# Projecting q, k and v of a tile in one stage, with 64-row remainders in pairs, in a vision-transformer block on one Trainium2 core

## The chip, the core and the metric

The kernel runs on one core of one Trainium2 chip. The metric is the time of one launch on the device in microseconds (us). The kernel before took 1381.76 us, the median of three runs (1381.58 to 1386.32). A core has five engines with a queue each: TensorE (PE, with its weight loads shown as PEld), VectorE (DVE), ScalarE (ACT), GpSimd (POOL) and SyncE (SP), which issues most transfers. Each engine works its own instructions off in the written order and waits on semaphores that others raise.

## The reference

64 images of 3x224x224 become 14x14 patches of 768 values. One transformer block follows, 12 heads of 16 channels, with layer norms; its feed-forward part rounds activations and weights to small integers.

```python
hidden = einsum('npd,hd->nph', patches, W_lin) + b_lin     # 768 -> 192
h = concat([cls_tok, cls_token, hidden])                   # 198 tokens an image
q, k, v = split(layernorm(h) @ w_qkv.T, 3)                 # 192 -> 576
q, k = rope(q * scale), rope(k)
out = softmax(q @ k.T) @ v                                 # 12 heads of 16
h = h + out @ w_proj.T + b_proj
up, gate = split(bitlinear(layernorm(h), w_in, g_in), 2)   # 192 -> 2 * 512
h = h + bitlinear(silu(gate) * up, w_out, g_out)           # 512 -> 192
```

## The kernel before

The 64 x 198 tokens are one row of 12672, cut into 99 tiles of 128 tokens. Attention works by image: 3 groups of 4 heads each, 192 groups in all. A loop over steps `s` (119 of them) stands in the program of each engine; a step embeds tile `s` (on PE `embed`, L427: 6 chunks of 128 rows by 192 columns) and works on earlier tiles and images at the same time. `half_steps` gives the half step at which each group's scores are maximised (`MAX_AT`), exponentiated and weighed (`EXP_AT`) and at which an image is normalised (`OUT_AT`); `projection_steps` gives the step of the feed-forward part of a tile (`PROJ_AT`). The order of the stages within a step is written out by hand at the end of each engine's program.

The way of a tile: PE embeds it, DVE adds the bias (L841) and takes the statistics (L845, L847), POOL normalises (`norm_x`, L984 to L991), PE transposes it (L437) as two blocks of 96 channels, ACT copies them to `xT` (L643), a ring of five images. `project_qk` (L446) makes q and k: two products over 96 rows each, 384 columns wide. `project_v` (L501) makes v by image: four products of 192 columns for the two halves of 99 tokens, since `weigh_values` (L513) needs the values of an image with its tokens on partitions 0 to 98. POOL turns q and k (`rotate`, L1003 to L1010), PE transposes them (L456), ACT copies (L661), POOL rounds a copy (L1019). PE multiplies scores for the row maximum (`max_scores`, L469) and again for the exponential (`exp_scores`, L490), for four heads at once, each on 32 of the 128 rows of the array; `weigh_values` puts four heads on 32 columns each. The negated maximum goes through a transposition (L478), a copy (L668) and a transfer of SP (`place_max`, L342) into `qkT`. After that come L522 (transposed output), L862 and L866 (normalised), L532, `project_out` (L539, L540), the residual (L872), the quantisation, `transpose_xr` (L547), `ffn_in` (L558: two products over 96 rows for each of two halves of 512 columns, bf16), `tanh_gate` (L716), `gated` (L903, L909), `transpose_yr` (L566) and `ffn_out` (L576).

Both kinds of scores use one set of four accumulator banks in turn: `take_score` makes PE wait until DVE (L854) or ACT (L675) has read what was there. All other outputs go to four banks `turn`, given out by `take` in the order of the program: the bank that was used longest ago, after a wait for its last reader. Products in 4-byte floats are two MATMUL instructions each in the trace, products in bf16 and transpositions one.

After the last tile is embedded (step 98), `keep_busy` (L414) adds four idle products a step.

Of the kernel before, what the change touches and what calls it, by code (L numbers as in the profile page):

```python
# [14 lines left out]
IMGS = 64  # L15
# [9 lines left out]
DC = D // 2  # L25
HEADS = 12
# [20 lines left out]
XRING = 5 * TOKENS  # L47
# [30 lines left out]
VALUE_AT = [EXP_AT[GROUPS * b] - 2 for b in range(IMGS)]  # L78


def projection_steps():
    steps = []
    for i in range(TILES):
        steps.append(max(steps[-1] + 1 if steps else 0, (OUT_AT[final_image(i)] + 3) // 2))
    return steps
# [3 lines left out]
STEPS = PROJ_AT[-1] + 8  # L89
# [38 lines left out]
X_COPIES = copies(TILES, TILE, XRING)  # L128
# [10 lines left out]
def build(nc, ins, out):  # L139
# [3 lines left out]
    with ExitStack() as ctx:  # L143
# [10 lines left out]
        wqkv = sb("wqkv", [DC, 2, 3 * D])  # L154
        wproj = sb("wproj", [DC + 1, 2, D])
        win = sb("win", [DC, 2, 2 * FF])
        wout = sb("wout", [128, FC, D])
        winq = sb("winq", [DC, 2, 2 * FF], BF16)
# [6 lines left out]
        wabs = sb("wabs", [128, 2])  # L165
# [9 lines left out]
        xT = sb("xT", [DC, 2, XRING + TILE])  # L175
# [8 lines left out]
        vaug = sb("vaug", [TT, 2, 2, HEADS, 32])  # L184
# [22 lines left out]
        xiT = sb("xiT", [DC, TBUF, 2, TILE], BF16)  # L207
# [30 lines left out]
        margin_loaded = sem("margin_loaded")  # L238
        bias_loaded = [sem(f"bias_loaded{p}") for p in range(BBUF)]
# [10 lines left out]
        qk_ready = sem("qk_ready")  # L250
# [13 lines left out]
        v_ready = sem("v_ready")  # L264
        v_copied = sem("v_copied")
        pv_ready = sem("pv_ready")
# [32 lines left out]
        ATTN_LOADS = 16 * 4  # L299
        FFN_LOADS = 16 * 6  # L300
        SUM_STEP = 5
# [6 lines left out]
        def _(sp):  # L308
# [20 lines left out]

            def load_rope(i):  # L330
# [6 lines left out]

            def place_max(b):
# [5 lines left out]

            def store(i):
# [5 lines left out]
            load(0)  # L351
            load_bias(0)
            load(1)
            for i in range(1, BBUF):
                load_bias(i)
            for i in range(TBUF):
                load_rope(i)
            load(2)
            for s in range(STEPS):
                for i in tile_at(s + 1):  # L360
                    if beyond(i) > TOKENS - PATCHES:
                        load_margin(i)
                    if i >= BBUF:
                        load_bias(i)
                for b in range(IMGS - XSLOT):
                    if final_tile(b) == s - 1:
                        load(b + XSLOT)
                for i in tile_at(s - 2):
                    if i >= TBUF:
                        load_rope(i)  # L370
                for i in at(PROJ_AT, s - 7):
# [3 lines left out]
                for b in at(NMAX_AT, 2 * s + 1):  # L375
                    place_max(b)
            for p in range(TBUF):
# [3 lines left out]
        def _(pe):  # L381
# [3 lines left out]
            def take(use, size, freed, count):  # L385
# [7 lines left out]
                bank_of[use] = k  # L393
                return k

            def take_score(freed, count):
                if score_freed[0] is not None:
                    pe.wait_ge(*score_freed[0])
                score_freed[0] = (freed, count)

            score_freed = [None]

            def weight_sums():
                pe.wait_ge(setup_dve, 3)
                k = take("win", 1, weights_ready, 1)
                pe.matmul(turn[:, k, 0:1], ones[0:DC, :], wabs[0:DC, 0:1], start=True, stop=True).then_inc(wsum_ready, 1)
# [9 lines left out]
            def embed(i):  # L416
                if i == 0:
                    pe.wait_ge(loaded_embed, 16)
                    pe.wait_ge(x_zeroed, XSLOT + 1)
                for b in range(first_image(i), final_image(i) + 1):  # L420
                    pe.wait_ge(x_loaded[b % XSLOT], 16 * (b // XSLOT + 1))
# [704 lines left out]
```

## Time and profile before

| | us |
|---|---|
| median of 3 runs | 1381.76 |
| the profiled execution | 1382.6 |
| its span, first to last instruction | 1380.8 |
| PE busy | 1327.5 (96%) |
| POOL busy | 1012.3 (73%) |
| DVE busy | 975.0 (71%) |
| ACT busy | 904.8 (66%) |
| first embedding of the last tile to the end | 161 |

The mean granted clock of TensorE was 0.986 of full speed. Engines overlap, so the busy times don't add up to the span. A busy PE isn't PE at its peak: the time of a stage is best read as the distance from its first instruction to the first of the next stage.

### The profile page before, as it was taken

How to read it: one execution, taken by the hardware profiler on the slowest of the kernel's cores; microseconds unless marked ns; L12 is line 12 of the kernel's file. 1: busy time of each engine (PE TensorE's matmuls, PEld its weight loads, DVE VectorE, ACT ScalarE, POOL GpSimd, SP SyncE). 2: the span in 40 equal slices, each digit the busy share in tenths (PEclk: the TensorE clock that was granted, in tenths of full speed). 3: DMA queues.
4: the chain of work that ended last, by engine and by line, in shares of the span. 5: the costliest groups of instructions: out<-in, count | busy, mean ns of one | idle time of the engine just before them, and what ended most of it. 6: DMA issues, size and time to landing. Idle time of an engine off the chain costs nothing.

```text
span 1380.8 us, 37853 instructions
## 1 busy us (share of the span) xinstructions
PE 1327.5 (96%) x13274; PEld 980.4 (71%) x13274; DVE 975.0 (71%) x2318; ACT 904.8 (66%) x1606; POOL 1012.3 (73%) x1610
## 2 busy tenths in 40 slices
PE   3899999999999999999999999999999999999997
PEld 2666777777777777777777777777777777767666
DVE  0644777777777777777787777777777777777765
ACT  0145667676777776767767767767767776767664
POOL 2655777887777787877878877778778778877544
PEclk8899999999999999999999999999999999999999
DMA  5421112221121221222122111211111221100000
GB/s 156 109 51 47 34 50 59 58 55 37 53 62 36 58 53 43 54 67 55 39 60 56 53 41 49 64 53 39 52 49 46 65 58 32 44 12 11 11 15 22
DMA packets 127119, 69.28 MB, mean 50 GB/s; under 512 B 50741, under 2 KB 126358, under 8 KB 126838
## 3 DMA queue, kind: packets, MB, share of 16 engines
q1 hardware_dynamic: 125884, 64.08, 17.7%
q10 hardware_dynamic: 1050, 2.79, 0.7%
q8 instruction: 110, 1.80, 0.6%
q14 instruction: 75, 0.61, 0.2%
HBM read 56.48 MB, written 9.73 MB: 48 GB/s over the span
## 4 chain that ended last, share of the span: by engine, by line
PE 89%; DVE 3%; SPq 2%; DMA 2%; ACT 2%; issue 2%; POOL 1%; DVEq 0%; POOLq 0%; ACTq 0%
PE turn L427 14%; PE score L490 12%; PE turn L513 11%; PE turn L446 10%; PE turn L558 6%; PE turn L501 6%; PE score L469 5%; PE turn L456 4%; PE turn L566 4%; PE turn L539 3%; PE turn L522 3%; PE turn L437 2%; PE turn L540 2%; PE turn L576 2%; PE turn L547 2%
## 5 line engine op out<-in xcount | busy, mean ns | idle before, releaser
L854 DVE TENSOR_REDUCE nmax<-score 99x8 f32<-99x1584 f32 x192 | 346.9, 1807 | 77.4 <-PE score L469 77.3
L675 ACT ACTIVATE prob<-score 99x1584 f32<-99x1584 f32 x192 | 286.6, 1493 | 95.9 <-PE score L490 95.9
L1019 POOL CAST qkTr<-qkT 128x768 fp32r<-128x768 f32 (+15 forms) x114 | 110.2, 973 | 198.5 <-ACT qkT L661 198.5
L427 PE MATMUL turn<-wlin,xp 128*128 128x192 f32 x1188 | 220.1, 337 | 24.9 <-DMA xp<-in_x 17.5
L427 PEld LDWEIGHTS turn<-wlin,xp 128*128 128x128 f32 x1188 | 199.6, 197 | 30.7 <-issue 30.7
L490 PE MATMUL score<-qkT 17*99 17x198 f32 x3072 | 179.2, 347 | 4.6 <-DVE nmax L854 4.5
L513 PE MATMUL turn<-prob,vaug 99*32 99x198 f32 x3072 | 167.4, 337 | 0.0
L446 PE MATMUL turn<-wqkv,xT 96*128 96x384 f32 x396 | 156.5, 519 | 0.0
L490 PEld LDWEIGHTS score<-qkT 17*99 17x99 f32 x3072 | 115.8, 160 | 51.3 <-issue 50.3
L1024 POOL TENSOR_SCALAR ve<-mv 128x1 f32<-128x1 f32 x99 | 123.1, 1243 | 32.8 <-DVE mv L847 24.9
L1033 POOL TENSOR_TENSOR yg<-y,gout 128x512 f32<-128x512 f32 x99 | 125.8, 1271 | 9.7 <-ACT yr L737 8.2
L692 ACT ACTIVATE osb<-turn 128x198 f32<-128x198 f32 x192 | 64.7, 337 | 81.2 <-PE turn L513 79.3
L513 PEld LDWEIGHTS turn<-prob,vaug 99*32 99x32 f32 x3072 | 80.6, 109 | 41.3 <-issue 15.9
L903 DVE SCALAR_TENSOR_TENSOR ag<-th,turn 128x512 f32<-128x512 f32 x99 | 68.1, 688 | 58.2 <-ACT th L716 58.2
L1003 POOL TENSOR_TENSOR ropec<-qk,rope 128x384 f32<-128x384 f32 x99 | 99.3, 1003 | 10.7 <-ACT qk L651 10.5
L1010 POOL TENSOR_TENSOR qkp<-ropec,ropes 128x384 f32<-128x384 f32 x99 | 99.2, 1002 | 7.8
L446 PEld LDWEIGHTS turn<-wqkv,xT 96*128 96x128 f32 x396 | 69.1, 193 | 50.4 <-issue 24.8
L558 PE MATMUL turn<-winq,xiT 96*128 96x512 bf16 x396 | 101.6, 378 | 0.0
L1005 POOL TENSOR_TENSOR ropes<-qk,rope 128x384 f32<-128x384 f32 x99 | 100.4, 1014 | 0.0
L708 ACT ACTIVATE xiT<-turn 96x256 bf16<-96x256 f32 x99 | 37.6, 380 | 89.6 <-PE turn L547 89.6
L841 DVE TENSOR_TENSOR h<-turn,bias 128x192 f32<-128x192 f32 x99 | 35.4, 357 | 83.5 <-PE turn L427 64.0
L501 PE MATMUL turn<-wqkv,xT 96*99 96x192 f32 x512 | 93.9, 326 | 0.0
(98 smaller groups left out, 2694.2 us busy)
## 6 DMA issues: line engine op xcount, KB each, us to landing
xp<-in_x SPq DMA_DIRECT2D x64, 588.0 KB, 4.7
out<-h SPq DMA_DIRECT2D x99, 96.0 KB, 2.0
qkT<-nmaxT SPq DMA_DIRECT2D x192, 3.1 KB
bias<-in_added SPq DMA_DIRECT2D x30, 74.2 KB
win<-in_win ACTq DMA_DIRECT2D x1, 768.0 KB
wlin<-in_wlin ACTq DMA_DIRECT2D x1, 576.0 KB, 3.8
rope<-in_cos SPq DMA_DIRECT2D x30, 6.2 KB
rope<-in_sin SPq DMA_DIRECT2D x30, 6.2 KB
```

The lines of the kernel that those rows point to most:

```text
L427: last = pe.matmul(turn[:, k, 0:D], xp[:, c, place:place + TILE], wlin[:, c, :], start=(c == 0), stop=(c == KC - 1))
L446: last = pe.matmul(turn[:, k, 0:QK], xT[:, c, place:place + TILE], wqkv[:, c, 0:QK], start=(c == 0), stop=(c == 1))
L490: last = pe.matmul(score[0:TT, r, t * TOKENS:(t + 1) * TOKENS], qkT[rows, GROUPS + g, place + t * TT:place + (t + 1) * TT], qkT[rows, g, p ...
L501: last = pe.matmul(turn[0:TT, k, t * D:(t + 1) * D], xT[:, c, place + t * TT:place + (t + 1) * TT], wqkv[:, c, QK:3 * D], start=(c == 0), ...
L513: last = pe.matmul(turn[32 * r:32 * r + 32, k, 0:TOKENS], vaug[:, b % 2, t, hd, :], prob[:, t, hd, :], start=(t == 0), stop=(t == 1), skip ...
L558: last = pe.matmul(turn[:, k + half, :], xiT[:, i % TBUF, c, :], winq[:, c, half * FF:(half + 1) * FF], start=(c == 0), stop=(c == 1))
L675: act.activation(prob[:, :, 4 * g:4 * g + 4, :].rearrange("p t r n -> p r t n"), score[0:TT, :, 0:2 * TOKENS].rearrange("p r (t n) -> p r ...
L854: dve.tensor_reduce(nmax[:, b % 2, :, 4 * g:4 * g + 4].rearrange("p t r -> p r t"), score[0:TT, :, 0:2 * TOKENS].rearrange("p r (t n) -> p ...
L1005: pool.tensor_tensor(ropes[:, :].rearrange("p (h e f) -> p h e f", e=DH // 2, f=2), src[:, :, :, ::-1], sin, ALU.mult).then_inc(rope_parts, 1)
L1019: pool.tensor_copy(qkTr[:, :, place:place + n], qkT[:, :, place:place + n]).then_inc(qkT_rounded, 1)
L1024: pool.tensor_scalar(ve2[:, c], mv2[:, i % TBUF, 1:2], 1.0 + NORM_EPS, LN_EPS * NORM_EPS, ALU.mult, ALU.add).then_inc(norm2, 1)
L1033: pool.tensor_tensor(yg[:, i % 2, :], y[:, i % 2, :], gout[:, :], ALU.mult).then_inc(yg_ready, 1)
```

## The change

- `project` replaces `project_qk` and `project_v`. For each tile it makes two outputs in two banks, 288 columns each: q with the first half of v, k with the second half of v. The 192 channels are taken as 128 rows and 64 rows. `xT` and the weights now hold channels 0 to 127 in chunk 0 and channels 64 to 191 in chunk 1. Side 0 takes its 128 rows from chunk 1 and its remaining 64 from rows 0 to 63 of chunk 0; side 1 takes chunk 0 and rows 64 to 127 of chunk 1. So the two remainders lie on different halves of the array's rows.
- `ffn_in` is cut the same way: `whole` (two products over 128 rows, 512 columns) and `rest` (two over 64 rows).
- `rest_first` puts the remainders first if the stage just before ended with remainders; otherwise they come last.
- v is copied by tile (`copy_v`, with a 1 behind the 16 channels of each head) and moved by SP (`place_v`, 2 or 3 transfers a tile) to `vaug`, a ring of six images, with a head every 17 columns; `weigh_values` reads 32 columns from there.
- The transposed tile is used one step after its embedding, not three; scores start two steps earlier. `exps` runs a half step later after the maximum, `transpose_max` in the same half step as the last maximum.
- The order within a step is remade on every engine. On PE both `weigh_values` stand together, `transpose_yr` comes five steps after `project_out` (four before) and `ffn_out` seven (four before), `project` is near the end of the step.
- At the start the image and weights of the embedding are loaded in halves, SP loads images ahead of most biases, the attention's weights come in 19 loads instead of 4, and the loads of the feed-forward weights are issued in step 4 by ACT instead of at the start.

```diff
-            top.append(max(top[-1] + 1 if top else 0, 2 * (final_tile(b) + 5) + 2))
-        turn.append(top[-1] + 1)
+            top.append(max(top[-1] + 1 if top else 0, 2 * (final_tile(b) + 3) + 2))
+        turn.append(top[-1])
         for g in range(GROUPS):
-            soft.append(max(soft[-1] + 1 if soft else 0, turn[-1] + 1))
-        out.append(soft[-1] + 2)
+            soft.append(max(soft[-1] + 1 if soft else 0, turn[-1] + 2))
+        out.append(soft[-1] + 3)
...
+            def project(i):
+                pe.wait_ge(xT_copied, i + 1)
+                k = take(("qkv", i), 2, v_copied, i + 1)
+
+                def whole(start, stop):
+                    for side in range(2):
+                        last = pe.matmul(turn[:, k + side, 0:SIDE], xT[:, i % 2, 1 - side, :], wqkv[:, 1 - side, side, :],
+                                         start=start, stop=stop)
+                    return last
+
+                def rest(start, stop):
+                    for side in range(2):
+                        rows = slice(side * REST, (side + 1) * REST)
+                        last = pe.matmul(turn[:, k + side, 0:SIDE], xT[rows, i % 2, side, :], wqkv[rows, side, side, :],
+                                         start=start, stop=stop)
+                    return last
+
+                if rest_first():
+                    rest(True, False)
+                    whole(False, True).then_inc(qkv_ready, 1)
+                else:
+                    whole(True, False)
+                    rest(False, True).then_inc(qkv_ready, 1)
...
+            def place_v(i):
+                sp.wait_ge(v_copied, i + 1)
+                over = (TILE * (i + 1) - 1) // TOKENS - VRING
+                if over >= 0:
+                    sp.wait_ge(pv_ready, GROUPS * (over + 1))
+                for p, half, at, n in token_runs(i):
+                    b = (TILE * i + p) // TOKENS
+                    sp.dma_start(vaug[at:at + n, b % VRING, half, 0:VROW], vt[p:p + n, i % VSLOT, :])\
+                        .then_inc(v_placed[i % VSLOT], 16)
...
-            for s in range(STEPS):
+            for s in range(-2, STEPS):
                 if s == SUM_STEP + 1:
                     weight_sums()
-                for b in at(OUT_AT, 2 * s - 2):
-                    transpose_on(b)
                 for n in at(MAX_AT, 2 * s):
                     max_scores(n)
-                for i in tile_at(s - 3):
-                    transpose_xn(i)
+                for b in at(OUT_AT, 2 * s - 1):
+                    transpose_on(b)
                 for i in tile_at(s):
                     embed(i)
-                if s >= TILES + LATE:
-                    keep_busy(s)
-                for i in at(PROJ_AT, s - 1):
-                    transpose_xr(i)
+                for i in tile_at(s - 1):
+                    transpose_xn(i)
                 for b in at(OUT_AT, 2 * s):
                     transpose_o(b)
+                for i in at(PROJ_AT, s - 7):
+                    ffn_out(i)
                 for b in at(NMAX_AT, 2 * s):
-                    transpose_max(b)
-                for b in at(NMAX_AT, 2 * s + 1):
                     transpose_max(b)
                 for n in at(EXP_AT, 2 * s):
                     exp_scores(n)
                 for i in at(PROJ_AT, s):
                     project_out(i)
-                for i in tile_at(s - 5):
+                for i in tile_at(s - 3):
                     transpose_qk(i)
+                if s >= TILES + LATE:
+                    keep_busy(s)
+                for i in at(PROJ_AT, s - 2):
+                    transpose_xr(i)
+                for n in at(MAX_AT, 2 * s + 1):
+                    max_scores(n)
+                for n in at(EXP_AT, 2 * s - 2):
+                    weigh_values(n)
                 for n in at(EXP_AT, 2 * s - 1):
                     weigh_values(n)
-                for n in at(MAX_AT, 2 * s + 1):
-                    max_scores(n)
-                for n in at(EXP_AT, 2 * s):
-                    weigh_values(n)
-                for i in at(PROJ_AT, s - 4):
+                for i in at(PROJ_AT, s - 5):
                     transpose_yr(i)
-                for i in at(PROJ_AT, s - 1):
+                for b in at(OUT_AT, 2 * s + 1):
+                    transpose_o(b)
+                for i in at(PROJ_AT, s - 2):
                     ffn_in(i)
-                for b in at(VALUE_AT, 2 * s):
-                    project_v(b)
-                for b in at(VALUE_AT, 2 * s + 1):
-                    project_v(b)
                 for n in at(EXP_AT, 2 * s + 1):
                     exp_scores(n)
-                for i in tile_at(s - 3):
-                    project_qk(i)
-                for b in at(OUT_AT, 2 * s - 1):
+                for i in tile_at(s - 1):
+                    project(i)
+                for b in at(OUT_AT, 2 * s):
                     transpose_on(b)
-                for b in at(OUT_AT, 2 * s + 1):
-                    transpose_o(b)
-                for i in at(PROJ_AT, s - 4):
-                    ffn_out(i)
+                for b in at(NMAX_AT, 2 * s + 1):
+                    transpose_max(b)
```

## Rows read from the trace of the kernel before

**Rows 1.** Windows: stretch, length, PE PEld DVE ACT POOL busy, clock, DMA share, GB/s.
```profile
0.00:20.00 20.00, 3.61 (x12) 3.35 (x12) 1.21 (x8) 0.00 (x0) 5.12 (x15) 0.90 0.77 209
20.00:40.00 20.00, 12.47 (x42) 11.50 (x43) 2.70 (x9) 1.66 (x2) 3.08 (x8) 0.68 0.36 90
40.00:60.00 20.00, 16.03 (x89) 13.10 (x88) 12.35 (x20) 4.89 (x10) 16.23 (x20) 0.92 0.46 126
...
200.00:1190.00 990.00, 987.10 (x10105) 725.92 (x10105) 741.07 (x1773) 694.99 (x1239) 777.74 (x1231) 1.00 0.20 52
...
1340.00:1381.00 41.00, 30.96 (x194) 25.49 (x192) 25.33 (x85) 19.48 (x40) 19.25 (x43) 0.96 0.06 20
```
**Rows 2.** The longest of PE's waits from 200 to 1190 us: total, times, longest.
```profile
PE turn L478 <- DVE h L841: 1.1, 3, 0.4
```
**Rows 3.** Timeline of PE: embeddings of tiles 3, 20 and 96.
```profile
34.34 1.94 PE L427 MATMUL turn<-wlin,xp 128*128 128x192 f32 x5 [6.47 <-issue]
...
208.52 2.12 PE L427 MATMUL turn<-wlin,xp 128*128 128x192 f32 x12
...
1194.46 2.12 PE L427 MATMUL turn<-wlin,xp 128*128 128x192 f32 x12
```
**Rows 4.** Timeline of PE, one steady step: start, length, line, operands.
```profile
703.67 0.38 PE L547 MATMUL turn<-ident,xr 128*96 128x128 f32 x2
703.89 0.34 PE L478 MATMUL turn<-ident,nmax 99*12 99x99 f32 x2
704.15 0.93 PE L490 MATMUL score<-qkT 17*99 17x198 f32 x16
705.01 0.59 PE L539 MATMUL turn<-wproj,onT 96*128 96x192 f32 x2
705.44 0.49 PE L540 MATMUL turn<-wproj,onT 97*128 97x192 f32 x2
705.77 0.82 PE L456 MATMUL turn<-ident,qkp 128*128 128x128 f32 x6
706.52 0.88 PE L513 MATMUL turn<-prob,vaug 99*32 99x198 f32 x16
...
708.99 1.03 PE L558 MATMUL turn<-winq,xiT 96*128 96x512 bf16 x4
709.85 1.46 PE L501 MATMUL turn<-wqkv,xT 96*99 96x192 f32 x8
711.15 1.45 PE L446 MATMUL turn<-wqkv,xT 96*128 96x384 f32 x4
712.44 0.51 PE L532 MATMUL turn<-ident,on 99*96 99x99 f32 x4
```
**Rows 5.** Timeline of PE: a `project_qk` that follows scores.
```profile
686.45 1.56 PE L446 MATMUL turn<-wqkv,xT 96*128 96x384 f32 x4
687.85 0.49 PE L576 MATMUL turn<-woutq,yiT 128*128 128x192 bf16 x4
```
**Rows 6.** Windows of the scores at 704.15 alone: PE busy (instructions that touch it).
```profile
704.14:704.20 0.06, 0.05 (x4) 1.00 0.00 0
...
704.38:704.44 0.06, 0.06 (x8) 1.00 0.00 0
```
**Rows 7.** Timeline of PE near the end: scores, then the next use of their banks.
```profile
1303.99 0.93 PE L490 MATMUL score<-qkT 17*99 17x198 f32 x16
...
1306.62 0.43 PE L469 MATMUL score<-qkTr 16*99 16x198 f32 x8 [0.93 <-ACT prob L675]
```
**Rows 8.** Line of the copy of v: busy us, mean ns, idle before, releaser.
```profile
L683 ACT ACTIVATE vaug<-turn 99x384 f32<-99x384 f32 x64 | 31.4, 491 | 40.5 <-PE turn L501 40.5
```
**Rows 9.** Waits of SP's queue: total us, times, longest.
```profile
SPq L342 <- ACT nmaxT L668: 581.2, 64, 22.3
```
**Rows 10.** Timeline of SP at the start: transfers that it issues.
```profile
3.04 17.64 SPq L327 DMA_DIRECT2D bias<-in_added  x7
...
29.64 1.24 SPq L313 DMA_DIRECT2D xp<-in_x  x2
```

More of the change, by code:

```diff
@@ L263, in build @@
         exp_done = sem("exp_done")
-        v_ready = sem("v_ready")
         v_copied = sem("v_copied")
+        v_placed = [sem(f"v_placed{p}") for p in range(VSLOT)]
         pv_ready = sem("pv_ready")
@@ L328, in load_bias, with prepare @@
                         .then_inc(bias_loaded[i % BBUF], 16)
+            def prepare(i):
+                if beyond(i) > TOKENS - PATCHES:
+                    load_margin(i)
+                if i >= BBUF:
+                    load_bias(i)
+                for b in range(1, IMGS - XSLOT):
+                    if final_tile(b) == i - 2:
+                        load(b + XSLOT)
             def load_rope(i):
@@ L393, in take @@
                 bank_of[use] = k
+                before[0], latest[0] = latest[0], use
                 return k
@@ L493, in exp_scores @@
                 last.then_inc(st_ready, 1)
-            def project_v(b):
-                pe.wait_ge(xT_copied, X_COPIES[final_tile(b)])
-                k = take(("v", b), 1, v_copied, b + 1)
-                place = TOKENS * b % XRING
-                for t in range(2):
-                    for c in range(2):
-                        last = pe.matmul(turn[0:TT, k, t * D:(t + 1) * D], xT[:, c, place + t * TT:place + (t + 1) * TT],
-                                         wqkv[:, c, QK:3 * D], start=(c == 0), stop=(c == 1))
-                last.then_inc(v_ready, 1)
             def weigh_values(n):
@@ L507, in weigh_values @@
                 pe.wait_ge(exp_done, n + 1)
[L508 removed]
+                for i in range(TOKENS * b // TILE, final_tile(b) + 1):
+                    pe.wait_ge(v_placed[i % VSLOT], 16 * runs_loaded(i, VSLOT))
                 k = take(("pv", n), 1, o_copied, n + 1)
@@ new lines, in _ @@
+            act.wait_ge(setup_pool, SETUP_POOL)
+            for s in range(-2, STEPS):
+                if s == SUM_STEP - 3:
+                    load_ffn()
+                for i in tile_at(s - 2):
+                    copy_v(i)
+                for b in at(OUT_AT, 2 * s - 1):
+                    copy_onT(b)
+                for b in at(NMAX_AT, 2 * s - 1):
+                    copy_maxT(b)
+                for i in at(PROJ_AT, s - 5):
+                    round_y(i)
+                for i in at(PROJ_AT, s - 3):
+                    sum_squares(i)
+                for i in tile_at(s - 1):
+                    copy_xT(i)
@@ L930, in _ @@
             dve.memset(ones[:, :], 1.0).then_inc(setup_dve, 1)
-            for s in range(STEPS):
+            for s in range(-2, STEPS):
                 if s == SUM_STEP:
```

302 lines of the change are left out of this document (160 added, 142 removed).

## The prediction

> **What bounds the kernel now.** I read the windows first. From 200 to 1190 us PE is busy for 987.1 of 990 us at the full clock of 2.4 GHz, while POOL, the next, has 777.7 us [rows 1]. Then the waits: in that stretch the longest of PE's waits on another engine comes to 1.1 us in total [rows 2]. So three quarters of the span are PE's own work, and a microsecond taken from it there is one gained, until another engine's chain is late. The start differs: from 0 to 60 us PE is idle for 16.4, 7.5 and 4.0 us, 27.9 in all, and the clock is low in part [rows 1]. The last 41 us have 10.0 us idle. A steady step takes (1194.46 - 208.52) / 76 = 12.97 us on average, from the embedding of tile 20 to that of tile 96 [rows 3].
>
> **PE's columns.** The timeline gives the price of a stage as the distance to the next one [rows 4]. L446 holds four instructions of 384 columns and takes 712.44 - 711.15 = 1.29 us, so 0.84 ns a column and instruction (a product in 4-byte floats is two of them). L501, eight of 192 columns, takes 711.15 - 709.85 = 1.30 us. L558, four of 512 in bf16, takes 0.86 us, 0.215 each.
>
> Before, q, k and v cost a tile 1.29 + 64/99 x 1.30 = 2.13 us. After, the 128-row products are four instructions of 288 columns, 4 x 0.242 = 0.97 us. The remainders are four more, two sides at a time if row halves run side by side: 2 x 0.242 = 0.48 us. Sum 1.45, so 0.68 us less a tile, 67 us for 99. `ffn_in` goes from four instructions to two and a pair, three times 0.215: 0.215 less, 21 us.
>
> Do 64-row halves run side by side? No row shows one. The nearest is L490, four 32-row heads at once: 16 instructions of 198 columns would take 16 x 0.166 = 2.66 us in a row and take 0.86 [rows 4]. Within it four start at once (4 in the first 0.06 us) and the next four about 0.24 us on (8 touch the stretch from 704.38) [rows 6]: waves of four, in which the second pass of a head doesn't hold up the first pass of the next. Two row halves are the same with two members, and each side has its own bank. I take full overlap. The other end is none: 2 x 0.242 + 0.215 = 0.70 us a tile lost, 69 us.
>
> The Trainium skill ("TensorE: Matmul & The Clock Gate", Part 3) says that matmuls start and end strictly in program order. If the two passes of a side stand next to each other in the program, that makes three rounds of the pair instead of two in `project`, 0.24 us a tile. By it the sum would be 24 us higher. The waves of the scores speak against it.
>
> **Changes of array mode.** A stage of part-array products costs more than its columns. L490's four waves are 0.665 us and it takes 0.86, 0.19 more; L446 takes 1.40 us behind scores [rows 5] against 1.29 behind a full-array stage, 0.11 more; and 0.09 more stands ahead of scores (L456 takes 0.75 us for six products [rows 4], and at the price of L547, 0.22 for two, it would be 0.66). In and out together are 0.39 us, 0.195 a change. "TensorEngine Tiling (Array Packing)" of the Trainium skill, Key Properties, says that a change of mode drains the engine; it gives no time, and it is the rule that speaks against this change. What the price is here, the rows say.
>
> So I count changes in both orders of PE. Before, a steady step has in order 32-row, full, 32-row (exp), full, columns, 32-row, columns, full, 32-row (exp), full: 10 changes. After: 32-row, full, exp, full, 32-row, columns (both `weigh_values` together), full, 64-row, exp, full, 64-row, and then 32-row at once in one step of three, or by a full-array transposition first in two of three: 11 or 12. `rest_first` is nearly never true, since scores stand between the two stages with remainders. Over all steps, with the half steps that slip, the lists give 959 changes before and 1124 after. 165 x 0.195 = +32 us. A change from 64 to 32 rows isn't in the trace. At nothing, the 131 of these would take 26 us off; I take the full price, since columns to rows and back also costs (two `weigh_values` with scores between them).
>
> The full-array transpositions (L437, L547) now write 128 rows rather than 96 with the same columns: 0.
>
> **New waits in the steady part.** The pipeline is shortened and PE runs faster, so I laid out one step with the durations of the rows.
> - Score banks. After `exp_scores` starts, ACT starts 1.0 us later and takes 1.49; the next use of the banks came 1306.62 - 1303.99 = 2.63 us after, when it did wait [rows 7]. The new order puts 0.86 + 0.43 + 0.33 + 0.75 + 0.22 = 2.59 us between (L490, L539, L540, L456, L547) [rows 4]. A wait of 0.04.
> - `ffn_in` takes a bank that `copy_yiT` frees. In one step of three a transposition of the output lies between it and `transpose_yr`, and there the pair needs that bank some 0.4 us too early: 0.13 a step.
> - Transposed tile one step after embedding rather than three. DVE's and POOL's parts (L841 to L847, then `norm_factor` and L984 to L991 behind `round_qkT`) end about 0.5 us into the next step by this layout; PE asks for them at 2.3 to 2.9. Hidden, with about 2 us of slack. POOL's work is 777.7 / 990 of a step of 12.97, 10.2 us of the new 12.6, and it must still wait for the copy of `qkT` in the middle.
> - v by SP. ACT copies 192 columns a tile, where L683 copied 384 an image in 491 ns [rows 8]. Even at 491 that is 49 us for 31, 0.2 a step on an engine with 695 of 990 us busy; I take nothing. SP's queue waits 581 us for `nmaxT` [rows 9], so two or three more issues a step hide, also for the stores and image loads queued with them. The values are wanted four steps after they are copied; DMA share is 0.20. Without that cover each late transfer would stand ahead of `weigh_values`.
> In sum about 0.17 us a step, 76 + some 15 steps: +15 us. From below the waits can't be less than 0; from above I take 0.6 a step, 55 us, the point at which the slack of each chain is gone.
>
> **Start and end.** At the start SP hung 17.6 us in the issues of seven biases, and the third image was issued at 29.64 [rows 10]. After, the images stand ahead and 1.5 MB of feed-forward weights are out of the way, so tiles 1 to 3 can be embedded some 10 us earlier; but the attention's weights, 19 issues, are now needed at step 1 rather than 3. After that each tile hangs on POOL (rotation, rounding, norm), so PE idles there as before. Of the 27.9 us idle I take 12 back (bounds 0 and 22). The tail has the same number of steps; two more of them are light feed-forward steps that hang on a chain through all engines: +2 (bounds -3 and 8).
>
> **Sum.** -67 - 21 + 32 + 15 - 12 + 2 = -51. The profiled execution took 1382.6 us, its span 1380.8; the median is 1381.8. From the median: 1331 us.
>
> **Rivals.**
> 1. The pairs don't overlap at all. Speaks for it: no row has 64-row products. Against: the waves. Then -67 - 21 + 69 = -19, with 32 for the changes, 15 for waits and -10 at the ends: +18, 1400 us, slower. It decides where less than a quarter of the 0.70 us is hidden.
> 2. Program order binds within the fp32 pair: three rounds, +24 us, 1355. For: the two passes of a side use the same rows. Against: the waves.
> 3. The shortened chain (embedding, statistics, `norm_x` at the end of POOL's step, transposition in the next, `project`, `rotate`) is late in each step, or DVE behind `gated` frees `ffin`'s banks late. For: POOL has 10.2 us of work in 12.6. Against: 2 us of slack. At 0.6 us a step instead of 0.17: 1331 + 39 = 1370. If the chain sets the step at 12.97 us, it is about 1371 too, since only start and end gain.
> 4. The change from 64 to 32 rows is free, or the start gives 22: 1331 - 26 = 1305.
> 5. Beyond the layout: with a step of 13.3 us on waits of the remade order, 1400.
>
> **How the numbers follow.** Forecast as told (1315 to 1350): 0.56. Rival 4: 0.12. Rival 2: 0.07. Rival 3: 0.14. Rival 1: 0.06. Rival 5: 0.05. The range goes from rival 4 less the better start (1305 - 8 = 1297) to rival 3 (1372) and leaves out 0.14. A measurement of this kernel tells 0.5% (7 us) from no change. Faster by more: all of 4, 2 and the forecast, and most of 3 (0.10): 0.85. Within it: 0.04. Slower: 0.11.
>
> **What would show it.** In the profile after: `project`'s stage at about 1.45 us of columns plus about 0.3 for changes, and its four remainder instructions in two waves; `ffn_in` at 0.65 plus 0.2. Steady steps of 12.6 us on average. PE still above 97% busy from 200 us on, with waits for the exponential and for `copy_yiT` of about 15 us in all. Embedding of tile 3 at 24 us or earlier rather than 34.34 [rows 3]. It would be wrong if the remainders come one after the other, if PE waits for `xn` or for banks in every step, or if POOL's busy share goes to 90% and more while PE's falls.

## The result, and the profile after

The changed kernel takes 1357.6 us (median of 4, 1357.0 to 1358.4) against 1381.7 us beside it: a ratio of 0.982, interval 0.980 to 0.984. It is faster, by 24 us where 51 were forecast. Medians here and below are of fast runs: one execution with both halves on the same rows and one with twice the filler took over 1.5% more than the fastest of their kernels and are left out. The span of the profiled execution is 1356.2 us, the mean granted clock 0.974 (0.986 before).

The windows of the changed kernel (stretch, length, then busy us and instructions of PE, PEld, DVE, ACT and POOL, granted clock, DMA share, GB/s):

```profile
0.00:20.00 20.00, 8.05 (x29) 6.53 (x30) 2.10 (x11) 1.67 (x2) 6.67 (x19) 0.88 0.65 181
20.00:40.00 20.00, 17.55 (x99) 12.67 (x99) 3.71 (x10) 5.41 (x12) 14.67 (x23) 0.95 0.62 165
40.00:60.00 20.00, 12.94 (x67) 9.48 (x67) 7.94 (x11) 3.64 (x8) 8.73 (x13) 0.74 0.24 64
...
200.00:1190.00 990.00, 977.09 (x10295) 707.57 (x10293) 782.47 (x1825) 712.28 (x1295) 703.55 (x1273) 1.00 0.24 61
1190.00:1250.00 60.00, 55.47 (x581) 39.60 (x578) 42.47 (x99) 38.91 (x68) 37.94 (x61) 0.91 0.05 16
1250.00:1300.00 50.00, 42.85 (x433) 31.29 (x436) 29.39 (x79) 29.59 (x51) 15.23 (x32) 0.83 0.04 12
1300.00:1340.00 40.00, 30.33 (x203) 22.71 (x200) 29.11 (x93) 21.73 (x46) 18.95 (x41) 0.87 0.04 13
1340.00:1357.00 17.00, 14.30 (x98) 12.41 (x95) 5.72 (x17) 6.12 (x11) 4.64 (x12) 1.00 0.12 36
```

They answer to [rows 1]. The middle is as it was forecast to be: PE busy for 98.7%, at the full clock but for the ten us from 475 us on (granted 0.66). What is new is the end. Before, the stretches at the same times ran at the full clock:

```profile
1190.00:1250.00 60.00, 58.56 (x603) 42.32 (x601) 43.50 (x100) 42.36 (x77) 48.29 (x79) 1.00 0.05 13
1250.00:1300.00 50.00, 48.19 (x533) 34.49 (x530) 37.19 (x87) 36.44 (x60) 31.98 (x46) 1.00 0.03 10
```

The first question is where the stages stand. Timeline of PE in the changed kernel, part of a steady step (start, length, line, operands), which answers to [rows 4]:

```profile
705.97 0.59 PE L611 MATMUL turn<-winq,xiT 128*128 128x512 bf16 x2
706.50 0.39 PE L618 MATMUL turn<-winq,xiT 64*128 64x512 bf16 x2
706.81 0.93 PE L552 MATMUL score<-qkT 17*99 17x198 f32 x16
707.67 1.24 PE L494 MATMUL turn<-wqkv,xT 128*128 128x288 f32 x4
708.84 0.76 PE L501 MATMUL turn<-wqkv,xT 64*128 64x288 f32 x4
709.53 0.43 PE L531 MATMUL score<-qkTr 16*99 16x198 f32 x8
```

`project` is L494 and L501, 709.53 - 707.67 = 1.86 us from start to start. Of this 1.45 are columns, as forecast, and 0.41 belong to its changes of array mode (0.3 was expected there). `ffn_in` is L611 and L618, 706.81 - 705.97 = 0.84 us (forecast 0.65 + 0.2). The embedding of tile 20 starts at 216.9 us and that of tile 96 at 1174.4: a step of 957.5 / 76 = 12.60 us, the forecast's 12.6.

Do the two halves run at once? L501 holds the four remainder instructions of that stage. Its windows (stretch, length, PE and PEld busy with the number of instructions that touch it, clock, DMA share, GB/s):

```profile
708.90:708.96 0.06, 0.06 (x2) 0.06 (x4) 1.00 0.09 9
...
709.10:709.16 0.06, 0.06 (x2) 0.04 (x2) 1.00 0.10 10
709.20:709.26 0.06, 0.06 (x4) 0.00 (x0) 1.00 0.07 7
...
709.40:709.46 0.06, 0.06 (x2) 0.00 (x0) 1.00 0.10 10
```

Two instructions are under way from the first tenth of a microsecond on, four where one wave ends and the next begins, then two again: two waves of two.

**Where the 51 us went.** PE's idle time was 53.3 us and is 66.8. From 0 to 200 us it fell by 4.1 (34.7 to 30.6), from 200 to 1190 us it rose by 10.0 (2.9 to 12.9), behind 1190 us by 7.6 (15.7 to 23.3). PE's busy time fell by 38.1 us. The clock explains why not by more. Take for each window its length times what is missing of the full clock: behind 1190 us that was 1.6 us before and is 60 x 0.09 + 50 x 0.17 + 40 x 0.13 = 19.1 now, in the middle nothing and now 10 x 0.34 = 3.4, from 0 to 160 us 16.8 and now 13.8. So the work of PE fell by about 38.1 + 17.5 + 3.4 - 3.0 = 56 us (an estimate, since some of the low clock falls on idle time), where the sum had -67 - 21 + 32 = -56. In one line: work -56, middle +10 idle and +3 clock, start -4 idle and -3 clock, end +8 idle and +17.5 clock, together -24. The end costs 25 us where +2 were forecast.

The times of single tiles can't be compared in this way. Tile 20 is embedded at 216.9 us and was at 208.5, although steps are shorter, since the shortened pipeline has PE do more of the work (12 us by its busy time) ahead of that point; that work is then missing behind the last tile.

Timeline of PE in the changed kernel near the end (in brackets the idle time before, and who ended it):

```profile
1224.51 0.50 PE L643 MATMUL turn<-woutq,yiT 128*128 128x192 bf16 x4
1226.21 1.11 PE L552 MATMUL score<-qkT 17*99 17x198 f32 x16 [1.20 <-DVE nmax L929]
1227.24 1.01 PE L592 MATMUL turn<-wproj,onT 96*128 96x192 f32 x2
...
1237.53 0.43 PE L531 MATMUL score<-qkTr 16*99 16x198 f32 x8 [1.44 <-ACT prob L735]
```

The last tile has been embedded and projected by then. Between `max_scores` (L531) and the `exp_scores` (L552) whose banks DVE's row maximum frees, only L585 and L643 stand; PE waits 1.20 us. Behind the wait the clock is at the lower of its two levels, 1.2 GHz (0.84 is granted from 1220 to 1245 us): L592 takes 1227.24 to 1228.05, 0.81 us, where it took 0.43 in the steady step of before [rows 4]. `keep_busy` (L457), the filler, stands behind `transpose_qk` in the new order, past the scores. That gave the theory for the first experiment.

### The profile page after: what moved, and what is told of

It is laid out like the page before. It is cut to its first block, busy times and chain, and to the rows that moved or that the text cites. A ratio compares the mean times of both kernels' runs of the same rounds, so it can differ in the third digit from the quotient of the medians.

```text
span 1356.2 us, 38149 instructions
## 1 busy us (share of the span) xinstructions
PE 1289.4 (95%) x13160; PEld 937.5 (69%) x13160; DVE 998.7 (74%) x2319; ACT 899.5 (66%) x1629; POOL 898.8 (66%) x1610
## 4 chain that ended last, share of the span: by engine, by line
PE 85%; DVE 4%; SPq 3%; DMA 3%; ACT 2%; issue 2%; POOL 1%; ACTq 1%; DVEq 0%; POOLq 0%
PE turn L475 14%; PE score L552 11%; PE turn L566 10%; PE turn L494 8%; PE score L531 5%; PE turn L501 4%; PE turn L518 4%; PE turn L633 4%; PE turn L611 4%; PE turn L592 3%; PE turn L575 3%; PE turn L618 2%; PE turn L593 2%; PE turn L457 2%; PE turn L643 2%; PE turn L585 2%
## 5 line engine op out<-in xcount | busy, mean ns | idle before, releaser
L1094 POOL CAST qkTr<-qkT 128x768 fp32r<-128x768 f32 (+15 forms) x114 | 86.4, 764 | 206.6 <-ACT qkT L721 206.6
L552 PE MATMUL score<-qkT 17*99 17x198 f32 x3072 | 180.5, 349 | 6.5 <-DVE nmax L929 5.6
L1108 POOL TENSOR_TENSOR yg<-y,gout 128x512 f32<-128x512 f32 x99 | 137.2, 1386 | 34.3 <-ACT yr L797 20.6
L566 PE MATMUL turn<-prob,vaug 99*32 99x198 f32 x3072 | 151.0, 336 | 0.0
L552 PEld LDWEIGHTS score<-qkT 17*99 17x99 f32 x3072 | 116.6, 162 | 44.6 <-issue 44.0
L494 PE MATMUL turn<-wqkv,xT 128*128 128x288 f32 x396 | 125.1, 440 | 2.5 <-ACT xT L703 2.3
L566 PEld LDWEIGHTS turn<-prob,vaug 99*32 99x32 f32 x3072 | 90.9, 110 | 33.3 <-issue 2.4
L776 ACT ACTIVATE th<-turn,fxh 128x512 f32<-128x512 f32 x99 | 68.1, 687 | 54.3 <-PE turn L618 54.3
L518 PE MATMUL turn<-ident,qkp 128*128 128x128 f32 x594 | 83.5, 277 | 14.1 <-ACT vt L744 8.5
L494 PEld LDWEIGHTS turn<-wqkv,xT 128*128 128x128 f32 x396 | 68.4, 192 | 39.1 <-issue 25.2
L703 ACT ACTIVATE xT<-turn 128x256 f32<-128x256 f32 x99 | 38.0, 384 | 82.9 <-PE turn L485 82.9
L531 PE MATMUL score<-qkTr 16*99 16x198 f32 x1536 | 84.5, 293 | 8.6 <-ACT prob L735 8.4
```

Source lines behind the costliest of these rows:

```text
L494: last = pe.matmul(turn[:, k + side, 0:SIDE], xT[:, i % 2, 1 - side, :], wqkv[:, 1 - side, side, :], start=start, stop=stop)
L518: last = pe.transpose(turn[:, k + side, g * TILE:(g + 1) * TILE], qkp[:, i % 2, head:head + 4, :].rearrange("p h d -> p (h d)"), ident[:, :])
L531: last = pe.matmul(score[0:TT, r, t * TOKENS:(t + 1) * TOKENS], qkTr[rows, g, place + t * TT:place + (t + 1) * TT], qkTr[rows, GROUPS + g, ...
L552: last = pe.matmul(score[0:TT, r, t * TOKENS:(t + 1) * TOKENS], qkT[rows, GROUPS + g, place + t * TT:place + (t + 1) * TT], qkT[rows, g, p ...
L566: last = pe.matmul(turn[32 * r:32 * r + 32, k, 0:TOKENS], vaug[:, b % VRING, t, VHEAD * hd:VHEAD * hd + 32], prob[:, t, hd, :], start=(t = ...
L1108: pool.tensor_tensor(yg[:, i % 2, :], y[:, i % 2, :], gout[:, :], ALU.mult).then_inc(yg_ready, 1)
```

## Experiments

Unless said, each is the changed kernel with the edit shown. Ratios are against the kernel before, run beside it on the same chip (1381.9, 1381.4 and 1382.8 us in the three groups); "+" and "-" are against the 1357.6 us of the changed kernel.

### The filler ahead of the scores

```diff
                 for i in tile_at(s):
                     embed(i)
+                if s >= TILES + LATE:
+                    keep_busy(s)
...
                 for i in tile_at(s - 3):
                     transpose_qk(i)
-                if s >= TILES + LATE:
-                    keep_busy(s)
```

> The changed kernel with the four idle products of each step after the last embedding put where the embedding stood (between the first scores for the maximum and the scores for the exponential), instead of behind the transposition of q and k. Theory: the changed kernel loses at its end because PE there waits for the row maximum in front of exp_scores (0.8 to 1.5 us a step from 1224 us on) and the granted clock then falls to 1.2 GHz for stretches; filled at that place, the waits on the row maximum go and the clock stays at 2.4 GHz for most of 1220 to 1300: 8 to 20 us faster than the changed kernel, 1338 to 1350. Rival: the end hangs on the chains of the other engines and the low clock is only a companion, the idle moves behind exp_scores, where the idle products stood: within 3 us of 1357.6.

Measured: 1335.8 us (1335.1 to 1341.5), ratio 0.967 (0.965 to 0.969), -22. The same eight instructions, earlier in the step. The windows behind 1190 us, and the timeline of PE where the first wait stood:

```profile
1190.00:1250.00 60.00, 55.48 (x615) 39.39 (x618) 45.96 (x106) 43.14 (x76) 40.77 (x67) 0.97 0.06 16
1250.00:1300.00 50.00, 43.53 (x474) 32.09 (x480) 35.17 (x103) 32.79 (x62) 18.30 (x42) 0.97 0.05 16
```

```profile
1222.17 1.49 PE L457 MATMUL turn<-wlin,ident 128*128 128x192 f32 x8
...
1223.92 0.93 PE L552 MATMUL score<-qkT 17*99 17x198 f32 x16
1224.78 0.59 PE L592 MATMUL turn<-wproj,onT 96*128 96x192 f32 x2
```

No wait for the row maximum stands there now, L592 is at 0.43 us again, and the clock at 0.97 where it was 0.91 and 0.83. From the embedding of tile 98 to the end there are 136.3 us rather than 156.9; four other kernels below whose edits leave the end alone have 152 to 159. Behind 1190 us PE's idle time falls from 23.3 to 16.6 us and what is missing of the clock from 19.1 to 3.3. So 22 of the 25 us of the end are the place of the filler, 7 by idle time and 16 by the clock. The steady step is unchanged (12.59).

### Twice the filler in the new place

```diff
-KEEP = 4
+KEEP = 8
...
-                    pe.matmul(turn[:, k, 0:D], ident[:, :], wlin[:, c, :], start=True, stop=True)
+                    pe.matmul(turn[:, k, 0:D], ident[:, :], wlin[:, c % KC, :], start=True, stop=True)
```

> The changed kernel with eight idle products a step after the last embedding instead of four, at their place in the changed kernel (behind the transposition of q and k). It tells the place of the filler from its amount. Theory (the place decides: the wait for the row maximum lies in front of exp_scores and isn't touched by work behind it): the added work, 19 steps of 1.3 us, is paid in part, 5 to 20 us slower than the changed kernel, 1363 to 1378, even if the clock is a little higher. Rival (any activity lifts the clock, and the clock is the loss): 5 to 15 us faster, 1343 to 1352.

Measured: 1376.0 us (1368.1 to 1380.8), ratio 0.994 (0.992 to 0.996), +18. PE's waits for the row maximum behind 1190 us (total, times, longest), of the changed kernel and then of this one:

```profile
PE score L552 <- DVE nmax L929: 2.6, 3, 1.2
```

```profile
PE score L552 <- DVE nmax L929: 3.2, 3, 1.2
```

More filler behind the scores doesn't shorten the waits ahead of them, and the clock stays low (0.89 and 0.80 in the two windows). It is only more work: 180.4 us from the embedding of tile 98 to the end. With the run before it: the place counts, not the amount.

### Both remainders on the same rows

```diff
-                        rows = slice(side * REST, (side + 1) * REST)
+                        rows = slice(0, REST)
```

(the same in `ffn_in` with `half`; the second side then takes the channels of the first, so the values differ, the work doesn't)

> The changed kernel with both 64-row remainders on rows 0 to 63 of the array, in project and in ffn_in, so side 1 takes channels 64 to 127 a second time instead of 128 to 191 and the output is not the reference's; columns, weight loads and order are the same. Theory (the halves run side by side): the remainders then stand one after the other, project takes 0.48 us more and ffn_in 0.215 us more a tile, 69 us in all less what hides in waits: 1405 to 1427. Rival (they didn't overlap anyway): 1358.

Measured: 1423.5 us (1408.0 to 1424.4), ratio 1.026 (1.021 to 1.031), +66. Timeline of PE of this kernel:

```profile
695.52 0.60 PE L618 MATMUL turn<-winq,xiT 64*128 64x512 bf16 x2
696.06 0.93 PE L552 MATMUL score<-qkT 17*99 17x198 f32 x16
696.91 1.24 PE L494 MATMUL turn<-wqkv,xT 128*128 128x288 f32 x4
698.08 1.23 PE L501 MATMUL turn<-wqkv,xT 64*128 64x288 f32 x4
699.25 0.43 PE L531 MATMUL score<-qkTr 16*99 16x198 f32 x8
```

L501 takes 1.17 us against 0.69, L618 0.54 against 0.31: 0.71 us a tile, the 0.70 that the prediction named as the other end of its bound. Shortly after L501's start one instruction is under way, not two (window as above):

```profile
698.22:698.28 0.06, 0.06 (x1) 0.06 (x2) 1.00 0.08 26
```

This is what rival 1 would have looked like, and it would have been slower than before.

### The pairs one at a time: whole 96-row chunks

`project` with 96-row chunks of weights and transposed tile and no remainder (288-column outputs kept), and in another kernel the same for `ffn_in`:

```diff
-                if rest_first():
...
+                for side in range(2):
+                    for c in range(2):
+                        last = pe.matmul(turn[:, k + side, 0:SIDE], xT[:, i % 2, c, :], wqkv[:, c, side, :],
+                                         start=(c == 0), stop=(c == 1))
...
```

> The changed kernel with project over two chunks of 96 channels again, four products of 288 columns over the full array, no 64-row remainders; q, k and v are still one stage with v moved by SP, ffn_in keeps its remainders. It prices the remainders of project in place. By the forecast's terms 0.48 us of columns come back and 5/3 changes of mode of 0.195 go a step: +0.16 us, 16 us slower than the changed kernel, 1373. By the stages of the changed kernel (1.17 + 0.69 against 2.05 to 2.14) +0.2 a step: 1374 to 1380. Rival (a wait of another engine sets the step, and PE's part is slack): within 4 us of 1357.6.

Measured: 1377.3 us (1371.7 to 1379.8), ratio 0.996 (0.994 to 0.997), +20.

> The changed kernel with ffn_in over two chunks of 96 channels again, four products of 512 columns, project as it is. By the forecast's terms 0.215 us of columns come back and one change of mode of 0.195 goes: +2 us, 1360. By the stage of the changed kernel (0.53 + 0.32 against 0.96 ahead of scores before) +0.11 a step: 11 us slower, 1366 to 1370. Rival: the place of ffn_in behind transpose_yr waits for banks in one step of three, and that takes it up: within 3 us of 1357.6.

Measured: 1372.1 us (1366.7 to 1378.3), ratio 0.993 (0.990 to 0.996), +14. Timelines of PE, first of the kernel with the whole `project`, then of that with the whole `ffn_in`:

```profile
708.24 2.21 PE L494 MATMUL turn<-wqkv,xT 96*128 96x288 f32 x8
710.28 0.34 PE L526 MATMUL turn<-ident,nmax 99*12 99x99 f32 x2
```

```profile
702.11 1.02 PE L611 MATMUL turn<-winq,xiT 96*128 96x512 bf16 x4
703.06 0.93 PE L552 MATMUL score<-qkT 17*99 17x198 f32 x16
```

Without the pair `project` takes 2.04 us against 1.86, 0.18 x 99 = 18 us of the 20 (it is 2.13 us where scores follow at once, in one step of three); `ffn_in` 0.95 against 0.84, 11 us of the 14. The steady step, 12.60 in the changed kernel, is 12.77 and 12.72: 17 and 12 us over 99 tiles. For `project` the prediction's own terms gave +16 (48 of columns less 32 for the changes): they hold. For `ffn_in` they gave +2, and +14 came. A pair in bf16 costs 0.31 - 0.215 = 0.1 us over its columns, the fp32 remainders 0.69 - 0.48 = 0.2, so one price of 0.195 for every change is too high for `ffn_in`. By the medians the pair of `project` is worth 20 us in all, that of `ffn_in` 14.

### Remainders always first

```diff
-                if rest_first():
-                    rest(True, False)
-                    whole(False, True).then_inc(qkv_ready, 1)
-                else:
-                    whole(True, False)
-                    rest(False, True).then_inc(qkv_ready, 1)
+                rest(True, False)
+                whole(False, True).then_inc(qkv_ready, 1)
```

> The changed kernel with the remainders of project always ahead of its 128-row products, so that they stand next to the exponential's scores. In the one step of three where scores follow project at once the number of changes of array mode stays; in the other two a full-array stage follows and one change goes. Theory (each change costs about 0.2 us wherever it stands): 99 x 2/3 x 0.2 = 13 us faster, 1343 to 1348. Rival (the price hangs on the pair of modes, and from 32 to 64 rows is dearer, or the waits for score banks take it up): 1352 to 1358.

Measured: 1350.9 us (1349.5 to 1359.3), ratio 0.979 (0.976 to 0.981), -7. Timeline of PE of this kernel:

```profile
706.18 0.76 PE L501 MATMUL turn<-wqkv,xT 64*128 64x288 f32 x4
706.86 1.24 PE L494 MATMUL turn<-wqkv,xT 128*128 128x288 f32 x4
708.03 0.43 PE L527 MATMUL score<-qkTr 16*99 16x198 f32 x8
...
730.74 0.76 PE L501 MATMUL turn<-wqkv,xT 64*128 64x288 f32 x4
731.43 1.24 PE L494 MATMUL turn<-wqkv,xT 128*128 128x288 f32 x4
732.50 0.34 PE L536 MATMUL turn<-ident,nmax 99*12 99x99 f32 x2
```

The sign was expected, since scores stand ahead of the stage and a transposition often behind, so a change falls away; half of the size came. Where scores follow, `project` takes 1.85 us as before (708.03 - 706.18). Where a full-array stage follows, it takes 732.50 - 730.74 = 1.76 us, and 734.09 - 732.24 = 1.85 in the changed kernel. So the change of mode that falls away is worth 0.09 us, not 0.2, and this is why only half came. The steady step is 12.55, 4.5 us over 99 tiles. The rest of the 7 isn't the edit's for sure: the intervals of this kernel and of the changed one overlap a little, and from the embedding of tile 98 to the end its profile has 152.3 us, but so has that of the kernel with the loads at the start (152.5), which is no faster in the median.

### A longer ring for the values of the tiles

```diff
-HRING = 20
+HRING = 24
```

> The changed kernel with 24 instead of 20 places for the tiles h, so that add_bias of a tile no longer waits for the store of the tile 20 before. Theory: the waits of VectorE for the store (15.5 us in 11 places, the longest behind the one step of 17.5 us) cost PE directly: steps above 14 us vanish, 5 to 10 us faster, 1348 to 1353. Rival: only the one long step counts, the others hide in VectorE's slack: 3 to 5 us, 1353 to 1355.

Measured: 1348.6 us (1344.7 to 1349.9), ratio 0.976 (0.974 to 0.978), -9. One step of the changed kernel takes 17.5 us (468.7 to 486.2). Timelines of SP's queue and of DVE there:

```profile
466.43 1.60 SPq L362 DMA_DIRECT2D vaug<-vt  x2
468.13 0.42 SPq L380 DMA_DIRECT2D out<-h  x1
```

```profile
474.20 0.36 DVE L916 TENSOR_TENSOR h<-turn,bias 128x192 f32<-128x192 f32 x1 [3.58 <-DMA out<-h]
```

DVE can't write the new tile until the store of the old one, in the same place of the ring, has landed. The store stands on SP behind the rotation tables and the two transfers of v. It is issued at 468.13 us, 2.5 us before DVE needs the place, and lands 6.0 us later, where the median of the 99 stores is 2.1. In total DVE waits 15.5 us, 11 times, for stores in the changed kernel; in the kernel before, with the same 20 places, it was 4.2 us, 4 times, and the slowest store landed after 4.4 us. With 24 places no such wait is left, no step is over 13.2 us, and the steady one takes 12.47. So the 9 us are the waits for stores. That v on SP's queue makes the stores late fits the order on SP, but no run takes v away from it, and the slow landing itself isn't explained by an issue that comes later. The prediction had put the stores at nothing ("hide, also for the stores ... queued with them").

### The start: more places for v, and the feed-forward weights at their old place

The longest wait of the start, on PE and on ACT, and SP's queue behind it (changed kernel, timelines):

```profile
47.97 1.51 PE L518 MATMUL turn<-ident,qkp 128*128 128x128 f32 x6 [6.67 <-ACT vt L744]
```

```profile
47.49 0.33 ACT L744 ACTIVATE vt<-turn 128x192 f32<-128x192 f32 x1 [8.58 <-DMA vaug<-vt]
```

```profile
39.44 3.83 SPq L352 DMA_DIRECT2D rope<-in_cos  x1
43.31 3.32 SPq L352 DMA_DIRECT2D rope<-in_sin  x1
...
50.13 1.51 SPq L362 DMA_DIRECT2D vaug<-vt  x2
```

Behind the issue of the feed-forward loads (31.7 to 35.3 us) SP hangs 3 to 4 us in each of three table transfers, v waits in the queue behind, the three slots of `vt` fill up, and ACT waits.

```diff
-VSLOT = 3
+VSLOT = 6
```

> The changed kernel with six places for copied v instead of three, so that copy_v no longer waits for the transfers of three tiles before. Theory: the wait of ACT for the transfer of v at 38.9 us (8.6 us, PE idle 6.7 us behind it, low clock afterwards) goes: 5 to 12 us faster than the changed kernel, 1346 to 1353. Rival: SP was held at 39 to 50 us by its own rope transfers behind the feed-forward weights, and rotate then waits for rope instead of copy_v for v: the gap stays, 1355 to 1359.

Measured: 1362.2 us (1362.0 to 1367.8), ratio 0.986 (0.984 to 0.989), +5 rather than a gain. ACT's wait is gone, and another stands in its place (timeline of PE):

```profile
61.45 1.66 PE L552 MATMUL score<-qkT 17*99 17x198 f32 x16 [6.10 <-DMA qkT<-nmaxT]
```

Tile 6 is embedded at 46.9 rather than 54.1 us, tile 20 at 221.4 rather than 216.9. The row of maxima goes through the same queue. It is issued at 58.1 us in both kernels, and SP has hung 5.8 and 3.3 us in table transfers at 40 and 46 us here too. So it looks as if SP's queue bounds this stretch, not the slots; why the median is 5 us higher isn't shown.

```diff
+            load_ffn()
...
-                if s == SUM_STEP - 3:
-                    load_ffn()
```

> The changed kernel with the nine loads of the feed-forward weights issued at the start again, behind the attention's, instead of in step 4. Theory: in step 4 these loads run into SP's own transfers (single rope issues of 3 to 6 us at 39 to 50 us), so v, rope and the maxima come late and PE idles 6.7 us and more between 40 and 80 us at the low clock; at the start they would sit behind the attention's weights, whose arrival at 16 us is awaited anyway. The wait at 41 us goes, the first 80 us get 5 to 10 us shorter: 1348 to 1353. Rival: at the start they delay the images and the attention's weights by as much (1.5 MB at 180 GB/s are 8 us), so the place doesn't matter: 1355 to 1361.

Measured: 1356.2 us (1351.9 to 1358.9), ratio 0.981 (0.979 to 0.983): no difference from the changed kernel. Yet the trace looks otherwise: from 37 to 55 us no table transfer holds SP for more than 1.6 us, one hangs 4.7 us at 21.5 us instead, and the wait of 6.7 us is gone. So the long hangs go with the feed-forward loads. Another wait stands in the place of the old one here too, 4.3 us of PE for the normalised tile. The place of the 1.5 MB is worth nothing that can be measured, though the prediction counted it among the reasons for the 12 us.

### The gains together

```diff
-HRING = 20
+HRING = 24
...
-                if rest_first():
...
+                if s >= TILES + LATE:
+                    keep_busy(s)
```

> The changed kernel with three edits together: idle products at the embedding's place, remainders of project first, 24 places for h. They gave 22, 7 and 9 us alone. Theory (they act in different stretches: end, every step, waits for stores): the sum, 1320 within 4 us. Rival (the waits for stores and for score banks take over what the remainders give): 1324 to 1330.

Measured: 1325.3 us (1318.7 to 1331.7), ratio 0.958 (0.954 to 0.961), -32 where the three alone sum to -38, in the range of the rival. But the rival's reason, waits that eat up the gain of each step, doesn't hold: the steady step is 12.42, 0.18 less, and the edits alone took off 0.05 and 0.12. The 6 us that are missing are small against the spread of the six runs, 13 us, in which the granted clock goes from 0.990 to 0.979 as the time rises. The kernel is faster than both others: 57 us below the one before.

To this a second set of filler between `project`'s place and `transpose_max`, in nine of the steps behind the last embedding:

```diff
+                if TILES + LATE <= s < TILES + 10:
+                    keep_busy(("p", s))
```

> The kernel of the three edits with a second set of four idle products in nine of the steps after the last embedding, at the place where project stood (behind the second exponential's scores), 1.3 us each. Theory: the waits for the exponential there (1.2 to 1.7 us a step) are filled at no cost and the clock stays up: 2 to 6 us faster than the kernel of three edits. Rival: what is awaited is a chain of ScalarE and VectorE, the filler only replaces idle time: within 2 us of it.

Measured: 1328.4 us (1323.2 to 1334.0), ratio 0.961 (0.958 to 0.964). PE's waits for the exponential from 1170 us on, without and with it:

```profile
PE score L527 <- ACT prob L731: 5.6, 5, 1.7
```

```profile
PE score L527 <- ACT prob L733: 1.5, 3, 0.6
```

The waits go, the clock is 1.00 from 1190 to 1250 us (0.91 without it), and the time doesn't fall. From the embedding of tile 98 to the end there are 139.3 us with it and 137.5 without: what the filler itself takes is as much as what it gives back. And the feed-forward loads at the start, on the same base:

> The kernel of the three edits with the feed-forward weights loaded at the start. Alone this gave 1.4 us of 1357.6 with a spread of 7. Theory: the start is set by the chain through POOL and by SP's queue alike, so it stays within 3 us of the kernel of three edits. Rival: with the waits for stores gone the start's gain shows, 5 us and more faster.

Measured: 1324.8 us (1321.6 to 1329.7), ratio 0.957 (0.955 to 0.960): no difference, as in the changed kernel.

## Why the prediction was right in sign and wrong in size

- **Columns, -67 and -21, and overlap of the halves: right.** Two waves of two in `project`, and +66 us when both halves stand on the same rows. Rival 1 had the right price and the wrong fact. Rival 2, the rule of strict program order in "TensorE: Matmul & The Clock Gate" (Part 3) of the Trainium skill as I applied it to the two passes of a side, falls: three rounds of 0.242 would be 0.73 us with no change of mode at all, and L501's stage takes 0.69 with its changes. Which side an instruction belongs to can't be seen in the trace, so the rule itself isn't tested, only my use of it.
- **Changes of mode, +32: right in sum, not as one price.** "TensorEngine Tiling (Array Packing)" of the Trainium skill, Key Properties, says that a change drains the engine, and the trace agrees that it costs time. The runs put it at about 0.2 us beside an fp32 remainder, 0.1 us beside a bf16 one, and 0.09 us for the one that falls away with remainders first. All work together fell by 56 us, as summed.
- **Waits of the steady part, +15: about right in sum (10.0 us, and 3.4 by the clock), wrong in kind.** The forecast named score banks and `copy_yiT`, 0.17 us a step. In the changed kernel none of PE's listed waits from 200 to 1190 us is for the exponential or for `copy_yiT`; 9 us of them are for DVE, in 15 places. A part of what came goes back to DVE's waits for stores, put at nothing. The longer ring gave 9 us back. The wrong sentence is the one on what hides SP's issues: 581 us of waiting in SP's queue [rows 9] is an average, and a single store can still be late.
- **End, +2: the step that failed.** The bounds were -3 and 8, and it cost 25. I counted the steps of the tail and how light they are, but in laying out the step I kept to the steady one, in which `embed` and `project` stand around the scores. Behind the last embedding they fall away, and `keep_busy`, the one stage that the kernel has for that place, had been moved behind the scores. [rows 7] showed the neighbour of this, a wait for the exponential of 0.93 us in the tail. And I priced a wait at its length: with the clock at 1.2 GHz behind it the work that follows costs double, and 17.5 of the 25 us are that.
- **Start, -12: mis-sized.** Tile 3 was embedded at 26.8 us (34.3 before; 24 expected) [rows 3], so the early tiles did come sooner. Idle time to 200 us fell only by 4 and the low clock by 3, as a part of the gain was lost again at 41 to 48 us, where v hangs behind the table transfers in SP's queue.
- **Rivals 3 to 5.** The shortened chain held: from 200 us on PE has no recurring wait for `xn`, and POOL's busy time fell (703.6 us of 990). The time of 1357.6 us lies in the stated range and close to rival 2's number, but by none of the rivals: it is the forecast's middle with a costly end. That the number fell into the range is luck, since the bounds of the end didn't hold it.

What stays open is the start. One wait was taken away and another took its place, twice. Transfers of v and of the maxima on another queue than the tables would test the reading; that wasn't tried, so the size of what the start could give isn't shown. Open too is why some stores land late.

## What to carry to other kernels

When an order is remade, lay out the step three times: filled, at the beginning and at the end, since a stage that only acts as cover in the last steps is easily moved past what it covers (22 us here for eight instructions a step in another place). Price a wait of TensorE together with the clock behind it, not at its length. What a queue carries is paid by the latest of its transfers, so count the slack of each (a ring of 20 or 24 places: 9 us), not the queue's mean idle time.

## What the runs showed of the hardware

- Two 64-row fp32 products on different row halves with outputs in different banks overlap wholly: 0.69 us for four instructions of 288 columns, 1.17 us if both are on the same half.
- The clock fell behind single waits of 0.8 to 1.2 us while PE was busy for 92% of the stretch (1190 to 1250 us, granted 0.91); a stage (L592) took 0.81 us in place of 0.43. Not every such wait does it: behind one of 0.89 us at 1214 us the next stages ran at the full clock. With the same work in another order it stayed at 0.97.
- A change of array mode has no one price: 0.09 us for the change that remainders first saves, about 0.2 us for the pair of fp32 remainders over its columns, 0.1 us for that in bf16.
- The issue of a table transfer on SP takes 0.25 us at 466 us and 3.83 us at 39 us, behind the feed-forward loads; with these loads at the start it takes at most 1.6 us there. It can also take 2.5 us in the steady part (at 471.6 us):

```profile
465.77 0.26 SPq L352 DMA_DIRECT2D rope<-in_cos  x1
466.08 0.25 SPq L352 DMA_DIRECT2D rope<-in_sin  x1
```
